# TensorE's order within a tile: the queries and keys, turned rows and output ahead of the weighted sums in first halves, the turned sums ahead of the weighted ones in second halves

## What is computed

```
x = x + attn(layernorm(x))           # q, k, v = x @ Wq, x @ Wk, x @ Wv; 16 heads
    scores = q . k_win * scale       # each row sees itself and the 63 rows before it
    ctx = softmax(scores) . v_win
    attn = ctx @ Wo
x = x + ffn(layernorm(x))
    scores = softmax(x @ w_router)   # two experts of eight for each row
    rows sorted by expert, 2048 slots for each; y = gelu(xb @ w1) @ w2
    out[row] += weight * y           # + bias
```

## Time and profile before

| | us |
|---|---|
| median of 3 runs | 908.19 (907.84 to 910.02) |
| the profiled execution's own time | 906.1 |
| its span, first to last instruction | 904.4 |
| TensorE busy | 761.4 |
| VectorE busy | 514.2 |
| ScalarE busy | 449.9 |

### The profile page before, as it was taken

How to read it: one execution, slowest core, us unless ns; L and a number is a source line. 1 busy time by engine, 2 the same in 40 slices (tenths; PEclk the granted TensorE clock), 3 DMA queues, 4 the chain that set the end, 5 groups by cost and what they waited for, 6 DMA issues and landing times.

```text
span 904.4 us, 19175 instructions
## 1 busy us (share of the span) xinstructions
PE 761.4 (84%) x7456; PEld 545.6 (60%) x7458; DVE 514.2 (57%) x1560; ACT 449.9 (50%) x916; POOL 354.0 (39%) x317
## 2 busy tenths in 40 slices
PE   8899999999999999999999997303999789798880
PEld 3556566566566566566565564202899679687780
DVE  3887887887887887877887876500212121211210
ACT  3656585585585586585585562001444243243320
POOL 2000000023222222223223143553478778678777
PEclk9999999999998999999999996555999999899895
DMA  2951100010100110100100111113255454555433
GB/s 67 365 220 34 33 8 13 27 34 26 48 29 23 39 38 27 50 30 26 48 29 29 45 39 32 62 41 120 19 85 80 79 105 58 79 105 60 81 33 32
DMA packets 48578, 54.21 MB, mean 60 GB/s; under 512 B 6001, under 2 KB 37384, under 8 KB 47472
## 3 DMA queue, kind: packets, MB, share of 16 engines
q0 software_dynamic: 22528, 17.22, 13.5%
q1 hardware_dynamic: 25968, 35.86, 12.0%
HBM read 17.70 MB, written 31.59 MB: 54 GB/s over the span
## 4 chain that ended last, share of the span: by engine, by line
PE 30%; DVE 30%; issue 17%; POOL 16%; DMA 5%; POOLq 1%; ACT 1%; DVEq 0%; SPq 0%; ACTq 0%
POOL out L435 14%; DVE kmax L658 6%; PE u_ps L1094 5%; DVE moving L672 5%; PE tail_ps L1078 4%; PE sT_ps L1069 3%; DVE negmax L664 3%; DMA out<-y_sb,xg 3%; PE sT_ps L1086 3%; DVE negmax_hl L669 3%; DVE ctx_sb L684 3%; POOL slots_dram L353 2%; DVE negmax_hi L667 2%; PE tail_ps L1114 2%; PE o_ps L1103 2%
## 5 line engine op out<-in xcount | busy, mean ns | idle before, releaser
L435 POOL DMA_INDIRECT out<-y_sb,xg x128 | 198.3, 1549 | 82.3 <-DVE y_sb L1003 42.8
L353 POOL DMA_INDIRECT slots_dram<-send_rows,slot_id x112 | 110.2, 984 | 172.4 <-PE sT_ps L1086 144.3
L509 ACT ACTIVATE probsT<-sT_ps 128x1024 f32<-128x1024 f32 x128 | 132.1, 1032 | 72.3 <-PE sT_ps L1086 70.3
L658 DVE TRANSPOSE_TENSOR_REDUCE kmax<-sT_ps 128x32 f32<-128x1024 f32 x128 | 159.4, 1245 | 9.9 <-PE sT_ps L1069 9.6
L590 ACT ACTIVATE hT<-sT_ps 128x512 f32<-128x512 f32 x128 | 76.6, 598 | 145.2 <-PE sT_ps L1284 137.3
L1069 PE MATMUL sT_ps<-qbd,kT 64*128 64x256 f32 x1024 | 133.3, 380 | 0.0
L368 POOL TENSOR_TENSOR xbias<-x_sb,bias_sb 128x256 f32<-128x256 f32 x32 | 23.4, 731 | 280.1 <-PE sT_ps L1086 272.5
L1284 PE MATMUL sT_ps<-xT_hl,w_hl 128*128 128x512 f32 x384 | 105.5, 427 | 20.0 <-DVE xT_hl L990 20.0
L1069 PEld LDWEIGHTS sT_ps<-qbd,kT 64*128 64x128 f32 x1024 | 98.5, 191 | 9.8
L1284 PEld LDWEIGHTS sT_ps<-xT_hl,w_hl 128*128 128x128 f32 x384 | 75.7, 204 | 37.2 <-issue 13.2
L990 DVE TENSOR_TENSOR xT_hl<-u_ps,xT_hl 128x512 fp32r<-128x512 f32 x32 | 22.1, 689 | 109.7 <-ACT xT_hl L583 109.7
(11 more groups left out here) (135 smaller groups left out, 1090.0 us busy)
## 6 DMA issues: line engine op xcount, KB each, us to landing
slots_dram<-empty_rows SPq DMA_DIRECT2D x8, 1096.0 KB, 14.8
xg<-slots_dram SPq DMA_DIRECT2D x32, 274.0 KB, 4.3
out<-xbias SPq DMA_DIRECT2D x32, 128.0 KB, 1.8
w_sb<-in_L_ffn_w SPq DMA_DIRECT2D x16, 256.0 KB, 3.2
send_rows<-rows_sb SPq DMA_DIRECT2D x7, 548.0 KB, 3.1
out<-y_sb,xg POOLq DMA_INDIRECT x128, 3.3
slots_dram<-send_rows,slot_id POOLq DMA_INDIRECT x112, 2.4
out<-empty_rows SPq DMA_DIRECT2D x1, 1024.0 KB, 19.8
```

The costliest lines, as they stand in the source:

```text
L353: pool.indirect_dma_start(out=slots_dram, out_offset=bass.IndirectOffsetOnAxis(ap=slot_id[:, k, j:j + 1].bitcast(U32), axis=0), in_=rows[: ...
L435: pool.indirect_dma_start(out=out, out_offset=bass.IndirectOffsetOnAxis(ap=xg[:, r, 4 * c + k, ROW - 1:ROW].bitcast(U32), axis=0), in_=y_s ...
L509: nc.scalar.activation(probsT[:, gp].rearrange("p b k h q -> p (b k h q)"), sT_ps[:, gp].rearrange("p b c -> p (b c)"), ACT.Exp).then_inc( ...
L658: nc.vector.tensor_reduce(kmax[:, u % 2, :], sT_ps[:, u % 2].rearrange("p b (c q) -> p (b c) q", q=32), AX.X, ALU.max, apply_transpose=Tru ...
```

## The change

TensorE, first halves: before, `shifted`, `weighted`, then the router or the counts where there are any and `project`, then `query_key` (odd tiles) or `normed_T` (even ones). Now, `shifted`, `query_key` or `normed_T`, then router or counts and `project`, and `weighted` last ahead of `maxima_T`. TensorE, second halves: `weighted_T` with its waits now stands ahead of `weighted`, and one wait that it makes needless is gone. ScalarE: in even tiles the copy `normed_T` (L477) goes ahead of `weighted_out`. No instruction, operand, buffer or DMA is added or removed.

```
@@ ScalarE, slot
                 exps(g, 0)
                 if t == 7 and not first:
                     gate_exps(b - 1)
+                if t % 2 == 0 and (t < 4 or not last):
+                    normed_T(b * PAIRS + (t + 4) // 2, (t + 4) // 2 % PAIRS)
                 if not (first and t == 0):
                     weighted_out(g - 1)
-                if t % 2 == 0 and (t < 4 or not last):
-                    normed_T(b * PAIRS + (t + 4) // 2, (t + 4) // 2 % PAIRS)
@@ TensorE, slot, first half
                 shifted(2 * g)
-                if done:
-                    pe.wait_ge(s_exp, 2 * g)
-                    weighted((t - 1) % TILES, 1)
+                if t % 2 == 1 and (t < 5 or not last):
+                    query_key(b * PAIRS + (t + 3) // 2, (t + 3) // 2 % PAIRS)
+                if t % 2 == 0 and (t < 4 or not last):
+                    n = b * PAIRS + (t + 4) // 2
+                    pe.wait_ge(s_v_sb, n - 1)
+                    pe.wait_ge(s_k_sb, n)
+                    normed_T(n, (t + 4) // 2 % PAIRS)
                 if left:
                     pe.wait_ge(s_ctxT_sb, g - 1)
...
                     project(g - 2)
-                if t % 2 == 1 and (t < 5 or not last):
-                    query_key(b * PAIRS + (t + 3) // 2, (t + 3) // 2 % PAIRS)
-                if t % 2 == 0 and (t < 4 or not last):
-                    n = b * PAIRS + (t + 4) // 2
-                    pe.wait_ge(s_v_sb, n - 1)
-                    pe.wait_ge(s_k_sb, n)
-                    normed_T(n, (t + 4) // 2 % PAIRS)
+                if done:
+                    pe.wait_ge(s_exp, 2 * g)
+                    weighted((t - 1) % TILES, 1)
@@ TensorE, slot, second half
                 shifted(2 * g + 1)
-                if t % 2 == 0:
-                    pe.wait_ge(s_v_sb, b * PAIRS + t // 2 + 1)
-                if done:
-                    pe.wait_ge(s_u, g)
-                weighted(t, 0)
                 if done:
                     if left:
                         pe.wait_ge(s_ctx, g - 1)
                     if t == 5 and not first:
                         pe.wait_ge(s_xn2T_sb, 2 * b)
                     weighted_T(g - 1)
+                if t % 2 == 0:
+                    pe.wait_ge(s_v_sb, b * PAIRS + t // 2 + 1)
+                weighted(t, 0)
```

## The result

The changed kernel takes 942.45 us in the median of 4 runs (941.35 to 944.4), beside 908.44 us for the kernel before (907.84 to 910.02). The ratio is 1.037, with a 95% interval of 1.035 to 1.040. The profiled execution has a span of 941.2 us (904.4 before). The attention stage makes all of the difference: its last half starts at 594.6 us, against 555.4, and what follows takes 2.4 us less than before.

What follows compares the result with a forecast made beforehand. No engine was taken to bound throughout: TensorE bounds odd tiles' halves, VectorE ends last in even tiles. Terms +5.8 + 1.5 - 2.2 - 0.9 - 1.6 - 3.0 = -0.4 us gave 907.8 (chance 0.50), range 904.0 to 912.0.

Steps and rivals of the forecast that it cites:

- The step that failed: Attention stage, GpSimd and SyncE: both only follow the instructions that release them, so they were counted as free.
- A: Tile 5, second half: L1103 waits for ScalarE's later copy L522 ahead of the weighted sums; +5.8 us together.
- B: Tile 1, first half: counts and output come later behind queries and keys; 0.25 in sequences 2 to 7, +1.5 us.
- C: Tile 6, first half: router and output L1114 come 0.30 earlier, and L693 follows; -2.2 us.
- D: Even first halves with little VectorE work: output L1114, which L693 waits for, comes 0.30 earlier; -0.9 us.
- E: Even second halves: L1103 comes 0.57 earlier for the reciprocal L680; 10 or 11 halves at 0.15, -1.6 us.
- F: TensorE, sums directly ahead of maxima: one change of array shape fewer in each half, 0.14 each; together -3.0 us.
- One change of shape saves nothing: Rival: the 0.14 belongs to every group, not to the change of shape; +3.2 us, 911.4; chance 0.27.
- The stall is small: Rival, tile 5: ScalarE's queue reaches L522 as early as now, so A costs 0.45 x 6; 905.1 us; chance 0.05.
- TensorE's clock stays up: Rival, tile 6: A's pause breaks unbroken work, so the clock's falls go; 3.2 us less, 904.6; chance 0.18.
- L1103's wait: Sign, tile 5's second half: L1103 waits for ScalarE's L522 seven times, about 0.9 us each in six.
- The sign that was to mean "wrong altogether": Odd tiles starting to wait for exponentials; the fill that waits for them was given 0.8 to 0.9 of room.

Runs made afterwards that it cites:

- e3: The changed kernel without GpSimd's 96 indirect sends of the attention stage: 897.35 us, beside 908.65 for the kernel before.
- e6: The changed kernel with GpSimd's sends of each half waiting for that half's weighted sums: 905.02 us, beside 903.71 for the kernel before.
- e3b: The kernel before without the 96 indirect sends of the attention stage: 901.14 us, a ratio of 0.993 to the kernel before.
- e11: The changed kernel with the old order in tile 5 and tile 1's first half (from sequence 2), sends behind the sums: 897.28 us, ratio 0.989.
- e2: The kernel before with the changed kernel's second halves on TensorE, first halves and ScalarE as before: 910.53 us, beside 908.65.
- e4: The changed kernel with first halves' weighted sums moved between queries and keys (or transposes) and router, counts and output: 961.18 us, beside 908.65.
- e12: The changed kernel with each group's eight weighted sums as full-array matmuls of 32 columns each: 1048.87 us, beside 907.83 for the kernel before.
- e10: The changed kernel with each group's eight weighted sums replaced by two full-array matmuls: 904.34 us, beside 907.13 for the kernel before.
- e5: The kernel before, in its own order, with GpSimd's sends held until the half's maxima: 910.48 us, beside 903.71.
- e8: The changed kernel with each attention-stage send replaced by a 128x256 addition on GpSimd: 905.11 us, beside 903.71 for the kernel before.
- e13: e11 with sends waiting for the sums only in first halves and in even tiles: 895.19 us, ratio 0.986 to the kernel before.

## Why the prediction was wrong, point by point

**The step that failed** is the sentence "GpSimd is released by L1086 and L693 ... both only follow". It is true of when GpSimd starts, and I stopped there. The question was what TensorE would now be doing while GpSimd sends. Before, the sums ran from 0.32 to 0.96 us of a half and the sends began at 1.19; after, the sums run from 0.91 (even tiles) or 1.92 (tile 1). I looked at each queue for order and never laid the sends' rows beside the sums' rows, although both were in the trace. That would have shown that they now meet, but not the price: no row of the kernel before has a late signal. What the runs showed in the step's place is that L664 starts 0.7 to 1.6 us late in the first halves with sends, and that the whole comes to 43.0 us (3.2 of them in tile 5's second half, where the clock fell), which are gone without the sends (e3); all but 5 are gone when the sends wait for the sums (e6). None of my cases had such a mechanism; the one that ended slower, a change of shape that saves nothing, stopped at +3.2. The loss was ten times that. Why a signal is late beside a send stays open.

The rest of the sum can be read from e3 against e3b, both without sends, added up over all halves of a kind:

- **A**, tile 5's second half: +6.2, forecast +5.8. In the changed kernel, sequence 4:

```profile
349.70 0.39 PE L1086 MATMUL sT_ps<-moving,ones 64*128 64x512 bf16 x2 [1.12 <-DVE moving L672]
350.23 0.63 ACT L522 COPY xn2T<-o_ps 128x512 f32<-128x512 f32 x1
350.96 0.63 PE L1103 MATMUL o_ps<-ident,u_sb 128*128 128x128 f32 x4 [0.87 <-issue]
351.52 0.64 PE L1094 MATMUL u_ps<-probsT,v_sb 128*32 128x128 f32 x16
351.98 0.40 PE L1078 MATMUL tail_ps<-ident,kmax 128*32 128x128 f32 x8
```

  L1103 stands still for 0.87 until the copy is over (350.86), as foreseen. In the changed kernel itself the half grows by 0.77 where the clock stays up.
- **B**, tile 1's first half: 0.34 in each of six, +2.0 instead of +1.5. I had taken 0.10 off the queries for the change of shape behind them. L1043 to L1135 measures 0.97 in the changed kernel (310.03 to 311.00), so nothing comes off.
- **C and D**: 0.40 to 0.47 where the clock was undisturbed in both (0.22 in one case), forecast 0.30 to 0.40. Without the clock's falls about -3.9 in sum, forecast -3.1.
- **E**: tile 4's second half -1.2 in sum, others of tile 0 -0.4, as forecast (-1.6).
- **F**: L1094 to L1078 is 0.46 (351.52 to 351.98), against 0.58; odd second halves -0.9, -1.0 and -0.3 in tiles 1, 3 and 7, handed back +0.6 in tile 2; first halves of tile 5 -1.3. The unit and the places were right. The parts of F as I listed them add up to -3.1, not -3.0.

All halves together differ by -2.4 with the clock's falls and by about -1.4 without them (three falls of 1.26 in e3b, two of 1.38 in e3); the forecast was -0.4. As a sum over what I had thought of, it holds to about 1 us, in part because errors offset each other: A and B came out 0.9 higher, C and D 0.8 lower.

**The rivals.** *One change of shape saves nothing* falls with F. *The stall is small* falls with A. *TensorE's clock stays up* falls too. The pause in tile 5 is there in e3, and the granted clock still falls in tile 6 of sequences 1 and 3. Window of tile 6 in e3, sequence 1, columns as in the earlier trace rows:

```profile
136.51:146.32 9.81, 9.05 (x93) 6.21 (x93) 6.10 (x22) 4.19 (x8) 0.00 (x0) 0.83 0.01 2
```

The falls change places from kernel to kernel: tile 6 of sequences 3 and 7 before, of 2, 3 and 4 in e3b, of 7 after, and none in e11. In the changed kernel three more have moved into tile 5's second half itself, the one with the pause, and cost 1.5 us each there, against 3.2 us for both falls before. So a pause doesn't keep them away. The Trainium skill, "TensorE: Matmul & The Clock Gate", Part 1, expects a clock that activity releases and idleness lowers. These rows bear out neither that nor my rival: the engine was busy 9.05 of 9.81 us in a window that shows 0.83, and in the changed kernel the half with the pause has a fall in three sequences and none in three.

Of what I had named as signs, L1103's wait, tile 5's second half (6.15 in e3) and the 0.46 came true. The sign that was to mean "wrong altogether", fills that wait for exponentials, was the wrong one to watch: it was the readers of TensorE's results that waited.

## What to carry to other kernels

When instructions are permuted within one engine, lay the new order beside what every other engine issues at that time, not only beside who waits for whom. If a reader starts well after the records that release it, in two engines at once, look for an indirect DMA issue on GpSimd next to it. A wait of the DMA issue on the end of the matmuls costs one line and took the ratio from 1.037 to 1.001 here. Then look at what the held work meets in its new place.

## What the hardware showed that I had not expected

**Late signals beside indirect sends.** While GpSimd issues indirect DMAs (0.98 us each), ScalarE and VectorE start on TensorE's results 0.4 to 1.6 us after the end of its records (up to 2.0 in sequence 7 of e2 and e4), more with many matmuls near the send. The late starts come at nearly fixed times after the first send's start, whatever the matmuls did: in tile 1 at +2.89 and +2.98 (after), +2.86 (e4), +2.87 and +2.97 (e12), +2.79 (e10), and in tile 0 at +2.11 (after) and +2.10 (e12). The second send ends at +2.27. Beside a send isn't the whole condition: in e2's tile 1 the sums end before the send, and in e5's they lie within it without a copy that is visibly late. The ends of matmuls are modelled in the trace, so whether the matmuls themselves or only their signals are late can't be told from it. The mechanism stays open, as does why maxima alone beside a send are on time in the kernel before.

The Trainium skill, "SBUF — State Buffer", section "SBUF: two separate sides", has VectorE and GpSimd shut each other out at a shared pair of ports, and gives TensorE and ScalarE ports of their own. That can't be this case, since ScalarE's copy is as late as VectorE's reading and the lateness goes with the number of matmuls. It does fit the second thing seen.

**VectorE's small work beside GpSimd's computing.** e8, sequence 4, tile 0, first half, then the same line L722 in the kernel before:

```profile
290.45 1.30 POOL L366 TENSOR_TENSOR junk<-bias_sb 128x256 f32<-128x256 f32 x2 [3.52 <-PE sT_ps L1096]
...
291.17 0.66 DVE L732 TENSOR_TENSOR r_oh<-erank,r_m 128x64 f32<-128x64 f32 x1
```

```profile
293.43 0.20 DVE L722 TENSOR_TENSOR r_oh<-erank,r_m 128x64 f32<-128x64 f32 x1
```

0.66 instead of 0.20, and it ends within 0.08 us of GpSimd's second addition (291.83 and 291.75). In e6 the held sends push GpSimd's `xbias` beside VectorE's work in tile 7:

```profile
356.02 0.82 POOL L368 TENSOR_TENSOR xbias<-x_sb,bias_sb 128x256 f32<-128x256 f32 x1
...
356.28 0.64 DVE L719 TENSOR_TENSOR r_t<-r_t,erank 128x64 f32<-128x64 f32 x1
```

L718, the same instruction, takes 0.23 in the kernel before. That is the 0.4 us of 7s in e6, e11 and e13. `xbias` is pushed back in the same way in 1s of e6 (1.18 to 1.94 us of the half, 4.65) and in 1s and 7s of e5 (from 1.75, 4.99).

**The price of a change of array shape** is 0.12 us here (0.58 to 0.46). Eight full matmuls of 32 columns take 1.8 us (e12), against 0.6 for two of 128 with as many columns in all (e10).
